# Cross attention and gated experts on one core: a new order of the attention step, with the output projection directly ahead of the value groups

## The reference

```
h = layernorm(x)
Q = h @ Wq.T + bq ; K = ctx @ Wk.T + bk ; V = ctx @ Wv.T + bv      # 16 heads of 16
scores = softmax(Q @ K.T / 4) ; o = scores @ V
x = x + tanh(g_xattn) * (o @ Wh.T + bh)
x = x + tanh(g_ffn) * experts(layernorm(x))                        # not touched
```

## Time and profile before

| | |
|---|---|
| median of three runs | 507.07 us (504.67 to 507.3) |
| profiled execution, its span | 509.6 us, 507.7 us |
| TensorE matmul busy | 487.7 us, 96% of the span |
| VectorE, ACT, POOL busy | 357.9, 266.6, 282.4 us |
| steps 1 to 14 of the attention | 57.79 to 245.67 us |
| last attention step and feed-forward net | from 245.67 us |

### The profile page before, as it was taken

One profiled execution on the slowest core, in us unless ns is written; L12 is line 12 of the kernel. 1 busy time (PEld: TensorE's weight loads), 2 busy tenths in 40 slices (PEclk: granted clock), 3 DMA queues, 4 the chain that ended last, 5 costly groups with the idle time before them and its releaser, 6 DMA issues.

```text
span 507.7 us, 11754 instructions
## 1 busy us (share of the span) xinstructions
PE 487.7 (96%) x4350; PEld 456.2 (90%) x4350; DVE 357.9 (70%) x768; ACT 266.6 (53%) x584; POOL 282.4 (56%) x339
## 2 busy tenths in 40 slices
PE   7888999999999999999899999999999999999996
PEld 6657999999999999997789999899999999999994
DVE  6866777877878877888577869856486456854444
ACT  4456766666676777667666533443335333233331
POOL 5645666666666666561676536644386444854440
PEclk9989999999999999999989999999999999999999
DMA  7793786677777777553601000010000100001001
GB/s 199 180 289 93 216 214 153 157 182 190 189 179 180 180 176 169 120 111 57 204 10 17 1 0 1 1 34 0 1 0 2 34 1 1 0 2 34 0 1 32
DMA packets 51144, 45.83 MB, mean 90 GB/s; under 512 B 33935, under 2 KB 40115, under 8 KB 51088
## 3 DMA queue, kind: packets, MB, share of 16 engines
q1 hardware_dynamic: 41310, 23.18, 19.6%
q0 software_dynamic: 7504, 18.69, 14.1%
q10 hardware_dynamic: 2274, 3.21, 2.0%
HBM read 20.59 MB, written 6.66 MB: 54 GB/s over the span
## 4 chain that ended last, share of the span: by engine, by line
PE 84%; DVE 6%; DMA 5%; issue 2%; ACT 2%; POOL 1%; ACTq 0%; DVEq 0%
PE bank L1368 14%; PE bank L1223 7%; PE bank L1246 7%; PE bank L1372 7%; PE bank L1385 6%; PE bank L1420 6%; PE bank L1205 6%; PE bank L1259 6%; PE bank L1193 5%; PE bank L1400 4%; DMA QS<-crow 3%; PE bank L1292 3%; PE bank L1403 2%; PE bank L1180 2%; PE bank L1335 2%
## 5 line engine op out<-in xcount | busy, mean ns | idle before, releaser
L970 DVE TENSOR_REDUCE nmax<-bank 100x1 f32<-100x361 f32 x256 | 130.0, 529 | 38.4 <-PE bank L1223 33.4
L419 POOL TENSOR_TENSOR awl<-hb,awh 128x400 fp32r<-128x400 f32 x63 | 70.2, 1114 | 109.4 <-ACT awh L627 109.4
L529 ACT ACTIVATE pt<-bank 120x400 f32<-120x400 f32 (+1 forms) x192 | 90.3, 503 | 25.8 <-PE bank L1246 12.2
L627 ACT ACTIVATE awh<-hb 128x400 fp32r<-128x400 f32 x64 | 34.5, 539 | 119.0 <-DVE hb L906 118.7
L1223 PE MATMUL bank<-KS,QS 96*100 96x362 f32 x256 | 86.9, 358 | 5.2 <-DVE nmax L970 4.8
L899 DVE TENSOR_TENSOR hb<-sil,bank 128x400 f32<-128x400 f32 x64 | 36.5, 570 | 73.7 <-PE bank L1385 37.9
L1246 PE MATMUL bank<-QS,KS 97*120 97x200 f32 (+1 forms) x384 | 66.4, 271 | 1.6 <-ACT pt L529 1.0
L1246 PEld LDWEIGHTS bank<-QS,KS 97*120 97x120 f32 (+1 forms) x384 | 60.2, 184 | 2.8 <-DMA QS<-crow 1.7
L328 POOL TENSOR_TENSOR cth<-craw,cth 128x724 fp32r<-128x724 f32 x16 | 27.7, 1729 | 63.0 <-ACT cth L475 54.8
L1223 PEld LDWEIGHTS bank<-KS,QS 96*100 96x100 f32 x256 | 41.6, 167 | 12.8 <-DVE nmax L970 7.3
L333 POOL DMA_DIRECT2D QS<-q_dram x90 | 46.0, 519 | 0.4 <-issue 0.3
(11 more groups left out here) (221 smaller groups left out, 1116.3 us busy)
## 6 DMA issues: line engine op xcount, KB each, us to landing
KS<-kn SPq DMA_DIRECT2D x128, 90.5 KB, 3.3
KS<-kn POOLq DMA_DIRECT2D x64, 90.5 KB, 3.4
craw<-ctxT POOLq DMA_DIRECT2D x14, 361.0 KB, 4.9
QS<-q_dram POOLq DMA_DIRECT2D x92, 50.0 KB, 3.6
q_dram<-qn ACTq DMA_DIRECT2D x4, 400.0 KB, 4.1
o_dram<-on SPq DMA_DIRECT2D x16, 100.0 KB
xr<-o_dram SPq DMA_DIRECT2D x16, 100.0 KB
y<-xs SPq DMA_DIRECT2D x8, 200.0 KB
```

The lines of the kernel that those rows point to most:

```text
L419: nc.gpsimd.tensor_tensor(awl[:, g % 2, slot], hb[:, slot], awh[:, g % 2, slot].bitcast(F32), ALU.subtract).then_inc(m["p_awl"], 1)
L529: nc.scalar.activation(pt[0:TW[t], u, :], pT[u % 3][0:TW[t], 0:CS], ACT.Exp, scale=float(DH) ** -0.5).then_inc(m["act_e"], 1)
L970: nc.vector.tensor_reduce(nmax[:, h // 8, pos % 8:pos % 8 + 1], pS[h % 2][0:S, 0:T], AX.X, ALU.max, negate=True).then_inc(m["dve_s"], 1)
```

## The change

In steps 0 to 13 all engines but SP and POOL get a new order; nothing is added or dropped. Step 14 keeps the old order as `late_step` on ACT, VectorE and TensorE (the conditions on `B - 2` move there), and step 15 is as before.

- **TensorE.** Unit 0 moves behind head 2, and the two halves of each key projection stand together. Units 1 to 3 stand ahead of `o_turn`. The value parts are split in other places. `y_proj` moves behind heads 14 and 15, directly ahead of the value groups; the third value part is ahead of these heads.
- **ACT.** `row_copy(i, 1)` comes ahead of the copy of osb and `row_send(i, 1)` behind it. `k_high(b, 0)` is ahead of `expo(i, 0)`, `ctx_high_of` right behind it (was last). `row_copy(i+1, 0)` is ahead of `expo(i, 6)`. `v_out(b, 2)` and behind it `row_send(i+1, 0)` come ahead of `expo(i, 9)`.
- **VectorE.** `shares` moves behind head 6. `variance` and `first_sum` come ahead of head 15.

```diff
 ACT body(i)
+                row_copy(i, 1)
                 if has_o(i):
                     ...
                     nc.scalar.activation(osb[:]..., pO[:, 0:CS], ACT.Copy).then_inc(m["act_o"], 1)
-                row_out(i, 1)
+                row_send(i, 1)
+                k_high(b, 0)
                 expo(i, 0)
-                if has_k(i):
-                    k_high(b, 0)
+                if has_c(i):
+                    ctx_high_of(i + 3)
+                k_high(b, 1)
                 expo(i, 1)
-                if has_k(i):
-                    k_high(b, 1)
                 expo(i, 2)
                 expo(i, 3)
                 expo(i, 4)
                 expo(i, 5)
                 wait(act, "pe_pv", i * UN)
                 v_out(b, 0)
+                row_copy(i + 1, 0)
                 expo(i, 6)
-                row_copy(i + 1, 0)
                 expo(i, 7)
-                if has_k(i):
-                    v_out(b, 1)
                 expo(i, 8)
+                v_out(b, 1)
+                v_out(b, 2)
+                row_send(i + 1, 0)
                 expo(i, 9)
-                row_send(i + 1, 0)
                 expo(i, 10)
                 expo(i, 11)
-                if has_k(i):
-                    v_out(b, 2)
-                if has_c(i):
-                    ctx_high_of(i + 3)
 VectorE body(i)
                 k_low(b, 1)
+                head(i + 1, 6)
                 if has_o(i):
                     shares(i)
-                head(i + 1, 6)
                 head(i + 1, 7)
 ...
                 head(i + 1, 14)
-                head(i + 1, 15)
+                if i >= 3:
+                    variance(i - 3)
 ...
                 elif has_y(i):
                     first_sum(i)
-                if i >= 3:
-                    variance(i - 3)
+                head(i + 1, 15)
 TensorE body(i), the new order whole (s = s_head(i+1, .), st = st_unit(i, .), k, v = k_part, v_part of b)
+ s0  s1  k(0, 0:3)  k(0, 3:6)  s2  st0  s3  k(1, 0:3)  k(1, 3:6)  s4  s5  st1  st2  st3  o_turn
+ s6  st4  s7  st5  v(0, 0:3)  st6  s8  v(0, 3:6)  s9  st7  row_turn(i+1, 0)  st8  s10  v(1, 0:3)
+ s11  on_turn  v(1, 3:6)  s12  st9  st10  s13  st11  v(2, 0:6)  s14  s15  y_proj  pv 0..11  row_turn(i+1, 1)
 for all three engines
-            for i in range(0, B - 1):
+            for i in range(0, B - 2):
                 body(i)
+            late_step(B - 2)
             last_step(B - 1)
```

More of the change, by code:

```diff
@@ L689, in body, with late_step @@
                         normed_x(0, k)
-                if i == B - 2:
-                    w_high(2)
-                    w_high(3)
+            def late_step(i):
+                wait(act, "pe_pv", i * UN)
+                wait(act, "pe_oT", i - 1)
+                nc.scalar.activation(osb[:].rearrange("p q s -> p (q s)"), pO[:, 0:CS], ACT.Copy).then_inc(m["act_o"], 1)
+                row_out(i, 1)
+                expo(i, 0)
+                expo(i, 1)
+                expo(i, 2)
+                w_high(0)
+                expo(i, 3)
+                expo(i, 4)
+                expo(i, 5)
+                tokens_high(0, 0)
+                expo(i, 6)
+                row_copy(i + 1, 0)
+                expo(i, 7)
+                w_high(1)
+                expo(i, 8)
+                expo(i, 9)
+                row_send(i + 1, 0)
+                tokens_high(0, 1)
+                expo(i, 10)
+                expo(i, 11)
+                w_high(2)
+                w_high(3)
             def last_step(i):
@@ L1071, in body, with late_step @@
                     root(0, 6)
+            def late_step(i):
+                head(i + 1, 0)
+                head(i + 1, 1)
+                head(i + 1, 2)
+                head(i + 1, 3)
+                head(i + 1, 4)
+                head(i + 1, 5)
+                shares(i)
+                head(i + 1, 6)
+                head(i + 1, 7)
+                quotient(i)
+                head(i + 1, 8)
+                tokens_low(0, 0)
+                head(i + 1, 9)
+                head(i + 1, 10)
+                head(i + 1, 11)
+                turned_o(i)
+                head(i + 1, 12)
+                tokens_low(0, 1)
+                head(i + 1, 13)
+                head(i + 1, 14)
+                head(i + 1, 15)
+                first_sum(i)
+                variance(i - 3)
             def last_step(i):
@@ L1530, in body, with late_step @@
+                if has_y(i):
+                    y_proj(i)
+                for u in range(UN):
+                    pv_unit(i, u)
+                second_rows(i + 1)
+            def late_step(i):
+                s_head(i + 1, 0)
                 st_unit(i, 0)
                 s_head(i + 1, 1)
[L1532 to L1538, removed]
@@ L1589, in body @@
                 s_head(i + 1, 12)
[L1590 to L1593, removed]
                 s_head(i + 1, 13)
                 st_unit(i, 11)
-                if has_y(i):
-                    y_proj(i)
+                y_proj(i)
                 s_head(i + 1, 14)
```

113 lines of the change are left out of this document (65 added, 48 removed).

## The result

Before: 507.03 us (median of 4 runs, 504.67 to 507.3). After: 516.02 us (4 runs, 515.53 to 516.45). The ratio is 1.0163, with an interval of [1.013, 1.0197]: 1.6% slower, where 510.1 was predicted, with a range up to 515.0. The profiled execution took 515.87 us (span 514.0), against 509.6 (507.7) before.

What follows compares the result with a forecast made beforehand. TensorE's queue, busy 96% of the span, was taken as the bound. Gains of 2.96 us against 6.0 of first-copy stalls gave +3.0: 512.6 profiled, 510.1 as median, since the median lay 2.5 below; range 503.2 to 515.

Steps and rivals of the forecast that it cites:

- The sign and the mechanism: Whole kernel: slower, +3.0 us, because first copies issued behind the context load land late at unit 0.
- 1.53 and 1.28: Stalls expected to go, in us: 1.53 at second copies (unit 6), 1.28 at third heads behind the roots.
- Issue and use: First copy: ACT sends it at T+10.25 (T is the row turn); unit 0 uses it at T'+1.59, next step.
- allowance: First copy, issue to landing: 4.43 us allowed before TensorE waits at unit 0, against 4.84 before.
- How long the copy then takes: First copies of steps 0 to 10: three at 5.36 us, eight at about 4.7; stalls 6.0 us in all.
- The two corrections that were netted to +0.8: First copies: later issue takes off up to 0.7 each, K-stack tail and o_dram write add as much or more.
- Step 4 of the working: In flight: 361 KB and up to 512 KB more issued 0.5 to 1.5 us ahead of the first copy.
- step 5: First copy's duration, taken from old second copies, which landed about with the context load; stalls 5.2 plus 0.8, 6.0 us.
- the copies queue behind everything: Rival: first copies wait for all loads ahead, 5.6 us each, 13.2 of stall, +10, 517 us; chance 0.10.
- The gains: Steps 0 to 13: second-copy stalls 1.53, root stalls 1.28 and a step 0 stall 0.15 go, 2.96 us.
- TensorE's order: Same matmuls reordered, projection ahead of the value groups: +0.01 us, bounds -0.1 to +0.1 a step, no cover needed.
- VectorE is the bound: Rival: copies in time, but 0.2 us a step lost at heads 8 to 11; 506.9 us, chance 0.04.

Runs made afterwards that it cites:

- e4: Changed kernel with POOL's eight weight loads moved from steps 3 to 10 into steps 11 and 12; 512.54 us, ratio 1.0103.
- e1: Changed kernel with the first copy's send moved ahead of `v_out(b, 2)`, the third value eviction; 507.7 us, ratio 1.0.
- e2: Changed kernel with ACT's `ctx_high_of(i + 3)` put back to the end of the step, the send still late; 513.14 us, ratio 1.0095.
- e5: Changed kernel with one wait added on POOL: weight and context loads go out only when the step's first copy has landed; 508.46 us, ratio 1.0017.
- e7: Changed kernel with the first copy sent ahead of the third value eviction and the projection put back ahead of heads 14 and 15; 508.87 us, ratio 1.0028.
- e6: Kernel before with only the projection moved behind heads 14 and 15, other engines in the old order; 515.33 us, ratio 1.0189.
- e8: Changed kernel with the context load cut in two, the second half issued only when the step's first copy has landed; 507.89 us, ratio 1.0012.
- e12: Changed kernel with earlier first send, step 14 reordered, and weight and context loads of steps 0 to 10 held for the first copy; 507.92 us, ratio 1.0014.
- e9: Changed kernel with the first copy sent ahead of the third value eviction and step 14 reordered on TensorE and VectorE; 505.91 us, ratio 0.9947.
- e11: Kernel before with the projection behind heads 14 and 15 and the third value tile's products split three and three around head 13; 512.08 us, ratio 1.0102.
- e10: Kernel before with the projection behind heads 14 and 15, all six third-tile value products behind unit 11, heads 11 and 12 adjacent; 513.4 us, ratio 1.0096.

## Why the prediction was wrong

The sign and the mechanism were right, the size was not. From row turn to row turn, steps 1 to 13 took 174.79 us before (57.79 to 232.58) and 183.24 in after (56.62 to 239.86): +8.45, where +3.2 was forecast (6.0 of stalls less 1.53 and 1.28). Of the 5.3 us missed, 4.1 are stalls of the first copy, 0.8 is the clean step (13.29 for 13.23) and 0.4 is left at the roots. The medians miss by 5.9: the profiled execution of before lay 2.5 above its median (1.6 of it in step 15), that of after at its median.

- *Issue and use* held: the send at T+10.0 (10.25 was worked out), the use 1.58 behind the row turn (1.59), the context load 0.31 ahead of the copy (it said near 1). The *allowance* was too short: 4.76 us by the steps' lengths, where 4.43 was worked out. That hid part of the next miss.
- *How long the copy then takes* is the step that failed. It took the second copies' times, three at 5.36 and eight near 4.7, mean 4.88. Measured are 5.14 where only the context load was ahead and 5.97 where weights were too; nine of the ten are waited for, and steps reach 15.1 us where 13.4 to 14.2 were forecast. Stalls came to 10.1 us over clean steps (0.55 in step 1, 9.55 behind it) against 6.0. The two corrections that were netted to +0.8 ("issued later behind the load" and "the tail of stacks and write") hid one large one: the old second copies had the context load ahead only, the new first copies have the weights too in steps 4 to 10, 0.6 to 1.2 us more on average. Step 4 of the working lists those 512 KB, and step 5 gives them no price. e4 prices them: with the weights gone the copies of steps 4 to 9 fall from 6.0 to 5.3 us. That loads issued just ahead are what makes the copy late is shown by e1, e2 and e5; how its time goes with their bytes is not settled. Step 5's reading that such a copy lands about when the context load does held: in after it lands from 1.1 us ahead of that load to 1.3 behind it. The rival "the copies queue behind everything" gave 5.6 us each and 517; it had the better price, and got 0.10.
- *The gains* of 2.96 were too high. The root steps came down from 13.95 and 13.72 to 13.60 and 13.36, 0.7 and not 1.28, though the reductions end where it said (first_sum at 210.81 = T+11.2). The second copies do not wait in steps 1 to 14 of after, where the stall at unit 0 gives them room; once that is gone, in e1, one waits again (5.73 us in the chain, step 1) and a few lose 0.1 to 0.3. The clean step is 13.29 and not 13.24. With the first copy mended the new order is worth 1.0 us in 12 steps of the profile and nothing in the medians.
- *TensorE's order* was priced at +0.01 a step with "cover: none needed". In the whole change that holds (e7). Its reason was wrong: e6 shows 0.42 a step when the projection goes without the value part taking its place.
- *VectorE is the bound*: not seen; TensorE has no idle of over 0.1 us ahead of a head in steps 1 to 13 of after, and VectorE's own idle for the heads' scores is 42.0 us (33.4 before).

The Trainium skill ("DMA: Bandwidth & Descriptors", Queues, rings and completion order) has two rules here, one that each DMA engine goes round the queues packet by packet, one that the semaphore's increment lands only behind all earlier writes of that engine. The traces agree with the second and give the first no help for the copy: its first landing event comes 1.05 to 1.43 us after the issue in every case looked at, its last up to 6.5 us after when the loads are ahead. What no run shows is whether the late share waits for its turn or only for its increment.

## What to carry over

When an edit makes a queue run earlier, list what that queue issues next and which small, awaited transfer it now overtakes. In these runs a copy of 3 KB landed late when hundreds of KB had gone out in the microsecond or two ahead of it, so send it first: one place earlier was worth 8 us here. Holding the load for the copy gave nearly as much, but made the queue that holds late for its other work. Before moving work away from between two uses of a bank, ask what it was covering.

## What was not expected

- A copy of 3.1 KB took 1.7 us alone (second copies in e8, by the trace), about 3.7 behind stacks and a write, 5.1 to 6.3 on average behind 361 to 873 KB more, and 7.0 in e12.
- In e12 an idle gap of TensorE of 2.03 us was followed by about 7 us at the lower clock, which cost about 3 us more (5.3 over a clean step, 2.3 of it the stall). The gaps of after in the attention steps, 1.55 us at most, had no such sequel (mean granted clock 0.997). The length of the gap alone does not tell: gaps of 1.03 us in e9, 1.11 in e11 and 1.49 in e10, near the end of attention, were followed by the lower clock within 2.2 us, for 3.4 to 6.8 us.
- The four medians of before lie between 506.48 and 507.97, single executions between 504.4 and 513.9; granted clocks from 0.98 to 1.0 go with them. An edit worth 1 us in the profile can't be seen beside that.
